# Low parts of the gelu values subtracted on GpSimd instead of VectorE

## What is computed

```python
xn = layernorm(x)
# first branch: a state-space layer, then an MLP
z  = xn + ssm_scan(rmsnorm(xn, scale1), A, B, C, D)
h  = rmsnorm(z, scale2)
h  = gelu(h @ w1 + b1, approximate=False) @ w2 + b2     # 512 -> 2048 -> 512
# second branch: a gated MLP whose inputs and weights are rounded to blocks of FP4
gate, up = fp4_linear(xn, w_gate), fp4_linear(xn, w_up)  # 512 -> 1408
out = x + (z + h) + fp4_linear(silu(gate) * up, w_down)
```

## Time and profile before

| | value |
|---|---|
| median of 3 runs | 3132.64 us (3131.24 to 3133.47) |
| span of the profiled execution, first to last instruction | 3132.1 us |
| TensorE (PE) busy | 3053.1 us, 97% |
| VectorE (DVE) busy | 2040.8 us, 65% |
| ScalarE (ACT) busy | 1086.7 us, 35% |
| GpSimd (POOL) busy | 1149.5 us, 37% |
| mean granted TensorE clock | 0.998 of full |
| L1239, the low parts, on DVE | 256 instructions, 178.3 us |
| L1237, the high parts, on DVE | 256 instructions, 110.8 us |
| hand-over between the halves | about 1727 to 1741 us |

### The profile page before, as it was taken

One profiled execution on the slowest core, in us unless ns is written; L12 is line 12 of the kernel. 1 busy time (PEld: TensorE's weight loads), 2 busy tenths in 40 slices (PEclk: granted clock), 3 DMA queues, 4 the chain that ended last, 5 costly groups with the idle time before them and its releaser, 6 DMA issues.

```text
span 3132.1 us, 43122 instructions
## 1 busy us (share of the span) xinstructions
PE 3053.1 (97%) x14861; PEld 2472.6 (79%) x14861; DVE 2040.8 (65%) x4427; ACT 1086.7 (35%) x1910; POOL 1149.5 (37%) x1097
## 2 busy tenths in 40 slices
PE   5899999999999999999999999999999999999999
PEld 3678888888877777777777788888888888888887
DVE  8798898987777776767777754444445444444442
ACT  5345655644544343343422422212222122221221
POOL 7556656655555545545554210110111111111000
PEclk9999999999999999999999999999999999999999
DMA  4133434356766666666644533333333333333320
GB/s 128 44 88 91 116 114 120 95 137 183 181 180 174 161 155 174 159 161 168 168 95 98 128 72 72 75 73 72 77 68 80 75 68 71 72 74 74 71 61 14
DMA packets 865577, 335.58 MB, mean 107 GB/s; under 512 B 680400, under 2 KB 771792, under 8 KB 862800
## 3 DMA queue, kind: packets, MB, share of 16 engines
q1 hardware_dynamic: 865360, 332.83, 43.4%
HBM read 225.21 MB, written 107.51 MB: 106 GB/s over the span
## 4 chain that ended last, share of the span: by engine, by line
PE 70%; DVE 15%; issue 5%; POOL 5%; ACT 2%; DMA 2%; SPq 1%; DVEq 0%; POOLq 0%; ACTq 0%
PE bank L880 22%; PE bank L896 22%; PE bank L757 14%; PE bank L779 7%; DVE qs L1000 3%; POOL qa L1547 2%; DVE qa L1017 2%; PE bank L820 2%; DVE qs L1011 2%; DVE qa L973 2%; POOL qa L1541 1%; DVE qb L1025 1%; PE bank L727 1%; PE bank L828 1%; DVE sg L965 1%
## 5 line engine op out<-in xcount | busy, mean ns | idle before, releaser
L880 PE MATMUL bank<-hT,Wp 128*128 128x512 f32 x3072 | 739.6, 390 | 2.2 <-DVE Wp L1188 2.2
L896 PE MATMUL bank<-Wp,G 128*128 128x512 f32 x3072 | 737.6, 389 | 0.0
L880 PEld LDWEIGHTS bank<-hT,Wp 128*128 128x128 f32 x3072 | 577.5, 188 | 122.6 <-issue 2.6
L896 PEld LDWEIGHTS bank<-Wp,G 128*128 128x128 f32 x3072 | 576.6, 188 | 119.9
L757 PE MATMUL bank<-XT,Wg 128*128 128x512 f32 (+1 forms) x2148 | 524.6, 393 | 6.8 <-DVE Wd L1032 6.8
L757 PE MATMUL bank<-XT,Wu 128*128 128x512 f32 (+1 forms) x2148 | 515.7, 389 | 15.9 <-DVE sg L965 15.7
L779 PE MATMUL bank<-Wd,HT 128*128 128x512 f32 x2112 | 515.4, 393 | 6.3 <-POOL HT L1555 5.0
L1237 DVE CAST G<-gf 128x512 fp32r<-128x512 f32 x256 | 110.8, 433 | 599.2 <-PE bank L896 580.0
L757 PEld LDWEIGHTS bank<-XT,Wu 128*128 128x128 f32 x2148 | 401.1, 190 | 106.7 <-issue 25.8
L779 PEld LDWEIGHTS bank<-Wd,HT 128*128 128x128 f32 x2112 | 391.9, 188 | 105.6 <-issue 15.4
L757 PEld LDWEIGHTS bank<-XT,Wg 128*128 128x128 f32 x2148 | 398.7, 190 | 95.9 <-DVE Wd L1032 8.8
(11 more groups left out here) (121 smaller groups left out, 2828.3 us busy)
## 6 DMA issues: line engine op xcount, KB each, us to landing
px<-in_L_attn_x_dram SPq DMA_DIRECT2D x128, 256.0 KB, 3.3
xin<-in_L_attn_x_dram SPq DMA_DIRECT2D x128, 256.0 KB, 3.3
sT<-r_K SPq DMA_DIRECT2D x128, 256.0 KB, 4.2
r_Z<-xin SPq DMA_DIRECT2D x64, 256.0 KB, 2.5
r_U<-ub SPq DMA_DIRECT2D x16, 1024.0 KB, 6.6
sU<-r_U SPq DMA_DIRECT2D x32, 512.0 KB, 5.0
r_Y<-sY SPq DMA_DIRECT2D x16, 1024.0 KB, 5.7
xl<-in_L_attn_x_dram SPq DMA_DIRECT2D x64, 256.0 KB, 3.1
```

What stands on the lines that cost most here:

```text
L880: ins = e.matmul(bk[:], Wp[f][wh][:, 0, k * P:(k + 1) * P], hT[xh][b % 2][:, k, :], start=(k == 0 and p_ == 0), stop=(k == KD - 1 and p_ = ...
L896: ins = e.matmul(ACC[j][:], G2[gh][:, n % 2, j * P:(j + 1) * P], Wp[f][wh][:, 1, :], start=(f == 0 and p_ == 0), stop=(f == 15 and p_ == 2))
```

## The change

The subtraction that makes the low part of the gelu values leaves VectorE's `gelu_parts` and becomes `gelu_low` in GpSimd's program. The instruction, its operands and its two semaphores are the same. On GpSimd the low parts of steps 0 and 1 stand ahead of `h_low(NW - 1)`. From n = 2 on, `gelu_low(n)` stands ahead of the step's `tile_z`.

```diff
@@ vector_program
                 e.tensor_copy(G2[0][:, n % 2], gf[:, n % 2]).then_inc(s_ghi, 1)
-                e.wait_ge(s_ghi, n + 1)
-                e.tensor_tensor(G2[1][:, n % 2], gf[:, n % 2], G2[0][:, n % 2].bitcast(F32), ALU.subtract
-                                ).then_inc(s_glo, 1)
@@ gpsimd_program
+            def gelu_low(n):
+                e.wait_ge(s_ghi, n + 1)
+                e.tensor_tensor(G2[1][:, n % 2], gf[:, n % 2], G2[0][:, n % 2].bitcast(F32), ALU.subtract
+                                ).then_inc(s_glo, 1)
+
...
+            gelu_low(0)
+            gelu_low(1)
             h_low(NW - 1)
             for n in range(2, 16 * NB + 2):
-                b, f = n // 16, n % 16
+                if n < 16 * NB:
+                    gelu_low(n)
                 for t, part in mlp_steps(n):
                     prepare(t, part)
```

## The result

The changed kernel took 3140.68 us (median of 11 runs, 3138.26 to 3144.14), the kernel before 3132.64 us (median of 11 runs beside it, 3131.24 to 3136.05). The ratio is 1.0025, with a 95% interval of 1.0016 to 1.0034: 8.0 us slower. Forecast were 3141.6 us and "slower".

The account below looks back on a forecast made before the run. PE's matmuls were taken to bound the kernel, with costs only at the hand-over. Two stalls with their slow clock, less an old wait, 6.4 + 4.8 + 1.7 - 3.9 = +9.0 us, gave 3141.6 us, range 3136.5 to 3145.5.

Parts of the forecast that it names:

- PE bounds the blocks, the move costs nothing there: From 1820 us on only matmuls set the time; POOL's longer subtractions hide in over 6 us of slack: zero.
- rival C: Block starts: POOL's subtraction holds up DVE's transposition, passing the 1.0 us margin 15 times: 3155 us, chance 0.06.
- First stall: Hand-over: `down(NW-1)` waits for `h_low(NW-1)`, now behind two subtractions on POOL: 4.7 us, at least 3.4.
- Clock: After each of PE's two new waits, the next 12 matmuls run at 1.2 GHz: 1.7 us more, bounds 0 and 1.7.
- T: Delay of SyncE's loads and `r_Z` stores behind the late `down(NW-1)`: 4.7 + 1.36 = 6.1 us, 3.4 at the low end.
- Second stall: `mlp2(3)` waits for `gelu_low(3)`, which stands behind the late `tile_z(4)` in POOL's queue: 4.8 us.
- The old wait: PE's 2.22 us wait for `w_low(6)` and 1.7 us of slow running behind it vanish: -3.9 us.
- The sum: Whole kernel: 6.4 + 4.8 + 1.7 - 3.9 = +9.0 us, giving 3141.6 us; bounds +4.6 and +12.5.
- The signs of being wrong: Wrong if L779 starts before 1742, `tile_z(4)` starts before 1761, or PE waits at block starts.
- The stated relation to the median: The median of the runs was said to lie 0.5 above the profiled 3132.1 us.
- Rival A: Hand-over: the clock stays full after both waits: +5.9 us, 3138.5 us, chance 0.13.
- Rival B: Hand-over: weight loads pace the `r_Z` stores, so `tile_z(4)` stays at 1757.49: +2.5 us, 3135.1 us, chance 0.09.

Follow-up runs that it names:

- Blocks 1 to 15 alone: Changed kernel, but VectorE keeps the subtractions of steps 0 to 15 and GpSimd makes those from step 16 on: 3132.86 us against 3133.20, ratio 1.0000.
- block 0 alone: Changed kernel, but GpSimd makes the low parts of steps 0 to 15 only, VectorE those from step 16 on: 3141.86 us, ratio 1.0025.
- second trace: The changed kernel run again with no edit, beside the kernel before: 3141.32 us against 3133.47, ratio 1.0025.
- early stores: SyncE's two `r_Z` stores moved right behind `w_load(11)`: on the kernel before 3129.34 us against 3133.20; on the changed kernel 3135.35 against 3133.03.

## Why the prediction was right

- **PE bounds the blocks, the move costs nothing there.** Right. Blocks 1 to 15 alone gave 1.0000 (0.9991 to 1.0009). In the trace after, POOL's subtraction starts 0.5 us after the cast and lasts 1.29 us, as priced. At block starts DVE's transposition comes earlier, not later (it follows the cast directly). It runs beside POOL's subtraction at its old 0.72 us, and `hT` is ready at 1907.35, 1.8 us ahead of the matmuls at 1909.12 instead of 1.0. In all blocks the transposition lasts 718 to 727 ns, and PE never waits from 1820 to 3120 us. So rival C falls. The timeline after, at the start of block 2:

```profile
1904.29 0.72 DVE L1221 STREAM_TRANSPOSE bank<-xl 128x512 f32<-128x512 f32 x1
1904.45 1.29 POOL L1635 TENSOR_TENSOR G<-gf,G 128x512 fp32r<-128x512 f32 x1 [4.15 <-DVE G L1237]
...
1906.22 1.13 DVE L1224 SCALAR_TENSOR_TENSOR hT<-bank,vec,hT 128x128 fp32r<-128x128 f32 x4 [1.21 <-ACT hT L1471]
...
1909.12 2.88 PE L880 MATMUL bank<-hT,Wp 128*128 128x512 f32 x12
```

- **First stall, 4.7 us.** Right in place and cause, too large by 0.7: 4.0 us in every trace that has two subtractions ahead. POOL's three instructions took 4.2 us, between the 3.6 of the lower bound (1738.37 to 1741.96) and the 4.9 of the upper (to 1743.3). They waited 1.0 us in all for VectorE's reads, where 1.7 were forecast.
- **Clock.** 1.7 us behind each wait were forecast, from the one costly wait of the kernel before. Measured were 1.6 and 1.5 us in one execution, 2.5 and 2.9 in another. The bound of 1.7 for a single wait was too small.
- **T = 6.1 us.** Too large. Counted from `mlp1(2)`, the stores were issued 4.2 us late in the first trace (1752.69 - 1734.35, against 1749.90 - 1735.71) and 5.1 in the second. The stall was 0.7 us shorter. And of the half clock's price 0.2 us fell on `down` in the first trace, where the clock fell behind `down`'s first matmuls, and 1.25 in the second, where 1.36 were forecast. On top of that the stores landed sooner, which T left out: `tile_z(4)` started 6.8 and 6.9 us after their issue, where it had been 7.6. So it came only 3.4 and 4.4 us late. The issue of the stores, before and after:

```profile
1749.90 1.08 SPq L536 DMA_DIRECT2D r_Z<-xin  x2
...
1752.69 0.90 SPq L536 DMA_DIRECT2D r_Z<-xin  x2
```

- **Second stall, 4.8 us.** Right in cause, mis-sized with T: 2.7 and 2.8 us, and 3.6 us in the trace of block 0 alone, where `tile_z(4)` came 5.3 us late. Experiments that move the stores or `tile_z(4)` take it away.
- **The old wait goes, -3.9 us.** Right, in both traces of the changed kernel.
- **The sum.** +9.0 were forecast, +8.0 and +7.9 measured. Waits sized some 0.7 and 2 us too large and a clock sized too small by up to 2 us cancelled. The places and causes were right; that the sum came within 1.1 us is in part luck. The profiled execution, at the cheap end of the clock, gives from `mlp1(2)` to `mlp1(7)` 38.8 us against 33.0 before, +5.8. The second gives +8.3.
- **The signs of being wrong.** Two of the three that the prediction names came up in the first trace: L779 started at 1741.23 us, before 1742, and `tile_z(4)` at 1759.49, before 1761. And the second wait, 2.7 us, lies under the 4 to 5.5 forecast. The second trace has 1743.02 and 1762.30 us. The signs were set as times from the start of the program, though `mlp1(2)` itself starts at other times in other executions (1733.17 to 1736.13 us in the traces of this case). Moved to the 1735.71 us of the kernel before, the first trace gives 1742.59 us, no longer early, and 1760.85 us, early by 0.15. What stays of the signs is the mis-sized T, not another cause.
- **The stated relation to the median** set a span against a median of run times. The profiled execution before was in fact 1.3 us above the median. The sum was a difference, so nothing hung on it.
- **Rival A** (full clock) falls: the clock was at 0.50 behind both waits. **Rival B** (stores that don't move with `down`) falls: they moved by 4.2 and 5.1 us, and `tile_z(4)` by 3.4 and 4.4, where the rival needed less than 1.3. What it says of the weight loads is half right. The early stores show that the place in SyncE's queue sets the issue, and that behind the weight loads the landing takes 4.7 us longer.

## What to carry to other kernels

Work that is moved to an idle engine takes a place in that engine's queue. Look at the instructions that it is put ahead of and those that it is put behind, at the stage changes first, where the engine is not idle. That POOL was idle for 63% in the mean said nothing about the 30 us in which it cost. And where an engine is held at a stage change, follow the wait back. Here a place in SyncE's queue was worth 3.9 us, the relief of VectorE nothing that could be measured.

## What the runs showed of the hardware

**The clock's price behind one and the same wait varies.** Five traces have the wait of 4.0 us at the hand-over. The half clock behind it cost 1.6 us in two of them (the changed kernel, and `tile_z(4)` behind `gelu_low(3)`) and 2.5 in three (the changed kernel's second trace, block 0 alone, and the changed kernel with early stores). In the three the granted clock stood at 0.50 before PE began again, in the two it was still full then, and fell within the next 2 us. One of each kind, the changed kernel's two traces, around PE's new start at 1741.23 and at 1743.02 us:

```profile
1741.00:1742.00 1.00, 0.77 (x3) 0.67 (x4) 0.00 (x0) 0.00 (x0) 0.17 (x1) 1.00 0.00 0
...
1742.00:1743.00 1.00, 0.00 (x0) 0.00 (x0) 0.39 (x1) 0.00 (x0) 0.96 (x1) 0.50 0.00 0
```

Behind waits of 2.7 and 2.8 us it cost 1.5 and 2.9. Behind 2.5 us in the trace of the kernel with blocks 1 to 15 it cost nothing:

```profile
1760.67 3.01 PE L880 MATMUL bank<-hT,Wp 128*128 128x512 f32 x12 [2.48 <-DVE Wp L1188]
```

In the kernel before 2.2 us had cost 1.7 us at the same line. What makes the clock fall sooner or later in an execution was not found out. One profile is a sample of it, and gave +5.8 us where the median of runs said +8.

**GpSimd and VectorE on the same SBUF read hold each other up both ways.** At the hand-over DVE's pair of subtractions took 3.42 us instead of 1.29, and POOL's two 3.04 instead of 2.58. After `tile_z(4)` the multiplication L1209 took 1.40 us instead of 0.49, as `gelu_low(3)` had started 0.15 us before it. It didn't matter there, as no wait of PE hung on L1209. The Trainium skill (SBUF — State Buffer, Who interferes with whom) says that GpSimd shares a pair of SBUF ports with VectorE's instructions in a two-port mode, and that the one that starts second is blocked for the whole instruction of the first. The trace agrees only nearly: POOL's ended at 1763.40 and L1209 at 1763.69, 0.29 us behind it, less than its 0.49. The same section says that a VectorE instruction with at most one SBUF input, outside the two-port modes, isn't held up at all. The transposition at 1904.29 agrees: it took its usual 0.72 us, and POOL's subtraction, begun 0.16 us behind it, its usual 1.29.
